# One strip of values and ones per head, and sums of the sixteen largest on VectorE, in a two-layer attention kernel

## The reference, cut to what matters

```python
# self-attention, in windows of 128 tokens
scores = jnp.einsum('bnqhd,bnkhd->bnhqk', q, k) / jnp.sqrt(jnp.float32(D))
attn = jax.nn.softmax(scores, axis=-1)
o = jnp.einsum('bnhqk,bnkhd->bnqhd', attn, v).reshape(B, L, C)
# cross-attention over the 16 largest scores of each head
top_s, top_i = jax.lax.top_k(scores, TOPK)
attn = jax.nn.softmax(top_s, axis=-1)
vg = jnp.take_along_axis(v_bh[:, :, None, :, :], top_i[..., None], axis=3)
o = jnp.einsum('bhqk,bhqkd->bqhd', attn, vg).reshape(B, L, C)
```

## Time and profile before

| | |
|---|---|
| median of 3 executions | 993.64 us |
| the profiled execution: its own time | 995.26 us |
| its span, first to last instruction | 993.2 us |
| mean granted TensorE clock | 0.979 |
| TensorE matmul busy | 899.6 us (91%) |
| VectorE busy | 755.2 us (76%) |
| ScalarE busy | 480.2 us (48%) |
| GpSimd busy | 223.9 us (23%) |

### The profile page before, as it was taken

The page is one execution under the profiler, slowest core; times in us unless marked ns, Lnnn a source line. Parts: engine busy times, 40 slices in busy tenths (PEclk is TensorE's granted clock), DMA queues, the critical chain, the costliest instruction groups (busy, mean ns, idle before and its releaser), DMA issues.

```text
span 993.2 us, 22268 instructions
## 1 busy us (share of the span) xinstructions
PE 899.6 (91%) x8160; PEld 652.8 (66%) x8160; DVE 755.2 (76%) x3952; ACT 480.2 (48%) x807; POOL 223.9 (23%) x169
## 2 busy tenths in 40 slices
PE   5978888998999899998999899998999987988997
PEld 3755656775678656775678665875668654774674
DVE  3669899897699866997589867998589865995423
ACT  3356554336462556527363556526463545534413
POOL 1226324020140405020140404111141302220101
PEclk9999998999999999999999999999999999898999
DMA  8304020000100120000100111000100100000000
GB/s 312 91 23 165 3 68 21 5 2 2 59 1 1 56 59 24 11 2 2 59 2 1 55 41 43 12 2 2 44 17 1 55 23 12 1 1 1 22 1 22
DMA packets 28651, 32.82 MB, mean 33 GB/s; under 512 B 4176, under 2 KB 25600, under 8 KB 28288
## 3 DMA queue, kind: packets, MB, share of 16 engines
q1 hardware_dynamic: 28544, 31.41, 9.9%
HBM read 25.05 MB, written 6.36 MB: 32 GB/s over the span
## 4 chain that ended last, share of the span: by engine, by line
PE 64%; DVE 23%; ACT 8%; issue 4%; DMA 1%; POOL 0%; SPq 0%; ACTq 0%; POOLq 0%
PE bank L1541 60%; DVE left L1243 6%; DVE negm L1206 5%; DVE top L1241 4%; PE bank L1743 2%; ACT hT L773 2%; PE bank L1559 2%; DVE negm L1268 2%; ACT arena L884 1%; DVE x L1180 1%; DVE stats L1122 1%; DVE xh L1134 1%; ACT arena L827 1%; DVE arena L1235 1%; DMA w_m<-in_w_ada 1%
## 5 line engine op out<-in xcount | busy, mean ns | idle before, releaser
L688 POOL TENSOR_TENSOR eS<-arena,top 128x1024 f32<-128x1024 f32 x32 | 62.0, 1939 | 276.3 <-DVE top L1241 276.3
L1541 PE MATMUL bank<-w_m,arena 128*128 128x256 f32 x512 | 112.6, 381 | 2.4 <-issue 2.4
L1541 PEld LDWEIGHTS bank<-w_m,arena 128*128 128x128 f32 x512 | 96.6, 190 | 16.8 <-issue 3.2
L1243 DVE MATCH_REPLACE8 left<-top,arena 128x64 f32<-128x64 f32 x512 | 99.8, 209 | 0.0
L1243 DVE MATCH_REPLACE8 left<-top,left 128x64 f32<-128x64 f32 x512 | 99.8, 208 | 0.0
L873 ACT ACTIVATE rden<-bank,chan 128x512 f32<-128x512 f32 x64 | 44.2, 690 | 106.5 <-PE bank L1541 106.4
L644 POOL TENSOR_SCALAR veps<-mv 128x4 f32<-128x4 f32 (+1 forms) x32 | 7.9, 247 | 366.2 <-DVE mv L1129 359.6
L827 ACT ACTIVATE arena<-bank 128x512 f32<-128x512 f32 x128 | 66.1, 602 | 46.3 <-PE bank L1541 46.3
L1206 DVE TENSOR_REDUCE negm<-bank 128x4 f32<-128x512 f32 x128 | 78.8, 681 | 12.5 <-PE bank L1541 11.7
L1241 DVE MAX8 top<-arena 128x8 f32<-128x64 f32 x512 | 67.7, 208 | 21.7 <-ACT arena L847 21.7
L1541 PE MATMUL bank<-qr,w_m 128*128 128x512 f32 x256 | 83.2, 406 | 0.2 <-ACT qr L783 0.2
(11 more groups left out here) (159 smaller groups left out, 1838.0 us busy)
## 6 DMA issues: line engine op xcount, KB each, us to landing
w_m<-in_w_m SPq DMA_DIRECT2D x4, 1024.0 KB, 5.8
xin<-in_x SPq DMA_DIRECT2D x4, 512.0 KB, 4.5
arena<-in_w_m SPq DMA_DIRECT2D x1, 2048.0 KB, 8.8
out<-x SPq DMA_DIRECT2D x4, 512.0 KB, 2.9
arena<-in_w_ada SPq DMA_DIRECT2D x1, 1536.0 KB, 10.4
gate<-gate_rows SPq DMA_DIRECT2D x12, 128.0 KB, 3.5
gated_bias<-gate_rows SPq DMA_DIRECT2D x12, 128.0 KB, 4.2
xin<-in_x SPq DMA_DIRECT2D x3, 384.0 KB, 3.1
```

The costliest lines, as they stand in the source:

```text
L688: nc.gpsimd.tensor_tensor(eS[:], S[:, t, :].rearrange("p (h n) -> p h n", h=H), top[:, :, 0:1].to_broadcast([P, H, LC]), ALU.subtract).the ...
L1243: i = nc.vector.match_replace(left[:, h, :], eight, scores, REPLACED)
L1541: return nc.tensor.matmul(dst, lhsT, rhs, start=start, stop=stop)
```

## The change

**Self-attention.** `vpad` becomes `vones`, in which each head has 16 values and 16 ones. Each of the 16 products of a window now stands by itself (no adding in pairs): it writes a strip of 32 partitions, 16 of them the weighted values and 16 the sum. The eight products with `ones_half` go, with their tile and its load. ScalarE's `self_denominator` goes. `window_divide` becomes four VectorE instructions, each waiting for the one before: a turn of 32x32 blocks of the whole bank (128x512) into `turned`, a reciprocal of the 16 sums of each query, a multiplication (128x256) into `quotient`, and a second turn (128x256) into `oT_self`. The bank counts as drained after the first turn. `project(1, a)` waits for the last turn (`s_self_out`).

**Top-k.** The sums are taken before the transposes. `exps` holds the exponentials of all 64 scores and of the 16 largest beside them, 1280 columns. A new GpSimd instruction `subtract_max_top` fills the latter after step 2, and `topk_exp` waits for both. Step 4 on VectorE first adds up the 16 (`tensor_reduce` of 128x256), inverts 16 sums, and then masks as before. A new GpSimd instruction `normalise_probs` (128x1024) multiplies the masked exponentials by the reciprocals, and only then may TensorE transpose them. In `values(2, b)` the products D go. ScalarE copies the products O to `oT` (`take_cross`), and Ln and Exp and VectorE's `cross_divide(2, b)` go. The second layer keeps its way.

**Orders.** `topk_exp(c, 1)` moves behind the fifth `silu`, `topk_exp(c, 3)` to the end of ScalarE's iteration, behind `cross_denominator(4, b)`; VectorE's `topk(c, 3, (4,))` moves behind `cross_divide(4, b)`, ahead of `window_divide(a, 3)`.

```diff
@@ window_divide, VectorE
             def window_divide(n, w):
                 key = ("PV", n, w)
-                dve.wait_ge(s_rd1, n * W + w + 1)
-                drain(nc.vector.tensor_tensor(oT_self[:, :, w * P:(w + 1) * P], ps(key)[:, 0:KC * P].rearrange("p (c n) -> p c n", c=KC),
-                                              rden_self[:, w % 2, :].rearrange("p (c n) -> p c n", c=KC), ALU.mult), key)
+                filled_wait(dve, key)
+                i = nc.vector.transpose(turned[:].rearrange("p h n -> p (h n)"), ps(key))
+                drain(i, key)
+                drained_wait(dve, key)
+                own.step(nc.vector.reciprocal(inverse[:], turned[:, :, D]))
+                own.wait()
+                own.step(nc.vector.tensor_tensor(quotient[:], turned[:, :, 0:D], inverse[:].unsqueeze(2).to_broadcast([P, H, D]), ALU.mult))
+                own.wait()
+                nc.vector.transpose(oT_self[:, :, w * P:(w + 1) * P],
+                                    quotient[:].rearrange("p (k n) d -> p k (n d)", k=KC)).then_inc(s_self_out, 1)
@@ topk, step 4, VectorE
                     if s == 4:
-                        dve.wait_ge(s_exp, n * W + t + 1)
-                        nc.vector.scalar_tensor_tensor(Sh, left[:], REPLACED, eS[:], ALU.is_equal, ALU.mult).then_inc(s_prob, 1)
+                        dve.wait_ge(s_exp, at + 1)
+                        if at:
+                            dve.wait_ge(s_prob, at)
+                        own.step(nc.vector.tensor_reduce(topk_sum[:], eS_top, AX_X, ALU.add))
+                        own.wait()
+                        nc.vector.reciprocal(topk_sum[:], topk_sum[:]).then_inc(s_sum, 1)
+                        nc.vector.scalar_tensor_tensor(Sh, left[:], REPLACED, eS, ALU.is_equal, ALU.mult).then_inc(s_masked, 1)
@@ GpSimd
+            def subtract_max_top(n, t):
+                pool.wait_ge(s_top16, n * W + t + 1)
+                nc.gpsimd.tensor_tensor(eS_top, top[:], top[:, :, 0:1].to_broadcast([P, H, TOPK]), ALU.subtract).then_inc(s_dif, 1)
+
+            def normalise_probs(n, t):
+                pool.wait_ge(s_sum, n * W + t + 1)
+                pool.wait_ge(s_masked, n * W + t + 1)
+                Sh = S[:, t, :].rearrange("p (h n) -> p h n", h=H)
+                nc.gpsimd.tensor_tensor(Sh, Sh, topk_sum[:].unsqueeze(2).to_broadcast([P, H, LC]), ALU.mult).then_inc(s_prob, 1)
@@ window_values, TensorE
                     for s in range(2):
                         for p in range(4):
-                            i = mm(ps(key)[32 * p:32 * p + 32, k * P:(k + 1) * P], vpad[:, w, 4 * k + p, 2 * D * s:2 * D * (s + 1)],
-                                   pT_self[:, w % 2, 4 * p + 2 * k + s, :], s == 0, s == 1)
-                for s in range(2):
-                    for p in range(4):
-                        i = mm(ps(key)[32 * p:32 * p + 32, KC * P:], ones_half[:, s, :],
-                               pT_self[:, w % 2, 4 * p + s:4 * p + 4:2, :], s == 0, s == 1)
+                            i = mm(out_of[32 * p:32 * p + 32, k, s], vones[:, w, 2 * (4 * k + p) + s, :],
+                                   pT_self[:, w % 2, 4 * p + 2 * k + s, :].rearrange("p (j n) -> p j n", j=RG), True, True)
@@ values, TensorE
-                    key = ("D", layer, n, k)
-                    fill_wait(pe, key)
-                    for p in range(4):
-                        i = mm(ps(key)[32 * p:32 * p + 32, :], pair_mask[:], pT[:, 4 * k + p, :], True, True)
-                    fill(i, key)
+                    if layer == 4:
+                        key = ("D", layer, n, k)
...
@@ full(a), ScalarE
                 for j in range(J):
                     silu(b, j)
-                    if j == 3:
+                    if j == 4:
                         exp_tables()
                         topk_exp(c, 1)
...
                 window(a, 1)
-                self_denominator(a, 0)
                 modulated(4, b)
                 window(a, 2)
                 last_query(b)
-                topk_exp(c, 3)
-                self_denominator(a, 1)
                 window(a, 3)
-                self_denominator(a, 2)
                 last_exps(b)
                 cross_denominator(4, b)
-                self_denominator(a, 3)
+                topk_exp(c, 3)
@@ full(a), VectorE
-                topk(c, 3, (3, 4))
+                topk(c, 3, (3,))
                 cross_divide(4, b)
+                topk(c, 3, (4,))
                 window_divide(a, 3)
```

More of the change, by code:

```diff
@@ L535, in _ @@
             load(head_select[:], t_in["head_select"], s_masks)
-            load(ones_half[:].rearrange("p s n -> p (s n)"), t_in["ones_half"], s_masks)
             load(pair_mask[:], t_in["pair_mask"], s_masks)
@@ L703, in _ @@
             layer_rstd(2, 0)
+            subtract_max_top(0, 0)
             add_bias(2, 0)
             gate_weight(1, 0)
+            normalise_probs(0, 0)
+            subtract_max(0, 1)
             add_bias(1, 1)
-            subtract_max(0, 1)
+            subtract_max_top(0, 1)
+            normalise_probs(0, 1)
             for i in range(2 * KC):
@@ L741, in _ @@
                     gate_weight(2, batch)
+                subtract_max_top(c, 3)
+                normalise_probs(c, 3)
                 layer_rstd(2, a)
@@ L747, in _ @@
             layer_rstd(3, b)
+            subtract_max_top(c, 0)
             add_bias(3, b)
+            normalise_probs(c, 0)
             subtract_max(c, 1)
+            subtract_max_top(c, 1)
+            normalise_probs(c, 1)
             subtract_max(c, 2)
+            subtract_max_top(c, 2)
+            normalise_probs(c, 2)
             subtract_max(c, 3)
@@ L807, in project_qk @@
                     biased(kT[:, k, :], ("qk", n, KC + k), CB["qk"] + KC + k)
-            def self_denominator(n, w):
-                key = ("PV", n, w)
-                filled_wait(act, key)
-                if w >= 2:
-                    drained_wait(act, ("PV", n, w - 2))
-                r = rden_self[:, w % 2, :]
-                own.step(nc.scalar.activation(r, ps(key)[:, KC * P:], ACT.Ln))
-                own.wait()
-                nc.scalar.activation(r, r, ACT.Exp, scale=-1.0).then_inc(s_rd1, 1)
             def window(n, w):
@@ L857, in take_probs, with take_cross @@
                                                    ps(key).rearrange("p (h q) -> p h q", h=4), ACT.Copy), key)
+            def take_cross(n, chunks=range(KC)):
+                for k in chunks:
+                    key = ("O", 2, n, k)
+                    filled_wait(act, key)
+                    drain(nc.scalar.activation(oT[:, k, :], ps(key), ACT.Copy), key)
             def cross_denominator(layer, n, chunks=range(KC)):
@@ L1406, in full @@
                 if a > 2:
-                    cross_divide(2, b)
                     first_moments(a)
@@ L1512, in last @@
                 last_max(b)
-                cross_divide(2, c)
                 residual_moments(2, c)
@@ L1723, in values @@
                     drained_wait(pe, ("TP", n, W - 1, k) if layer == 2 else ("B3", n, k, RG - 1))
-                    key = ("D", layer, n, k)
-                    fill_wait(pe, key)
-                    for p in range(4):
-                        i = mm(ps(key)[32 * p:32 * p + 32, :], pair_mask[:], pT[:, 4 * k + p, :], True, True)
-                    fill(i, key)
+                    if layer == 4:
+                        key = ("D", layer, n, k)
+                        fill_wait(pe, key)
+                        for p in range(4):
+                            i = mm(ps(key)[32 * p:32 * p + 32, :], pair_mask[:], pT[:, 4 * k + p, :], True, True)
+                        fill(i, key)
                     key = ("O", layer, n, k)
@@ L2133 @@
         "pair_mask": (r[:, None] // LC == np.arange(2 * D)[None, :] // D).astype(np.float32),
-        "ones_half": np.repeat(np.eye(2, dtype=np.float32), D, axis=1).reshape(1, 4 * D).repeat(P, axis=0),
     }
```

100 lines of the change are left out of this document (57 added, 43 removed).

## The result

The changed kernel takes 1025.0 us (median of 4 executions, 1022.41 to 1025.58). Beside it, on the same chip, the kernel before took 993.07 us. The ratio is 1.0315, with a 95% interval of 1.0286 to 1.0343. It is slower, and 12 us above the forecast of 1013.

The account below looks back on a forecast made before the run. It took TensorE (64% of the chain) and VectorE (23%) to bound the kernel together. Terms -11 - 1 + 20 + 7 + 7 - 3 = +19 us on 995.26 gave 1014, forecast as 1013; range 978 to 1036.

Parts of the forecast that it names:

- Costs of one: Single instructions: the new window_divide takes 1.7 us against 0.34, +1.4 per window; step 4's sum adds 0.6 per tile.
- the rival of slow turns: Window divisions: turns at their upper bound cost 0.79 us more per window, +20 us in all, 1033; chance 0.13.
- The new products: Windows' four-strip products: a rival had them not cheaper, 0.9 us more per window, at most +5, 1018; chance 0.03.
- Start of the iteration: values(2, b) to project(2, b): no products D or wait for Ln and Exp, 2.2 us gained; five iterations -11 us.
- MLP: MLP stretch: nothing lost; VectorE's two added sums (1.2 us) are covered by its 1.46 us wait there.
- Windows: Self-attention windows: VectorE's queue delays window(a, 3) by 2.2 us and project(1, a) by 3.3; six iterations +20 us.
- the block: Window division: VectorE's multiplication of SBUF operands stands still until GpSimd's normalise_probs is through, +1.0 us.
- Clock: After TensorE's gaps ahead of window(a, 3) and project(1, a): drops to 1.2 GHz cost 1.2 us per iteration, +7 us.
- Tail: Kernel's end, no windows: the projection behind cross_divide comes earlier, the last normalising stands open, -3 us.
- First two blocks and a = 2: Front: divisions, sums and waiting less a quarter of waits for ScalarE, +7, bounds 0 and +12; a = 2 -1.
- additions fit into idle time: Whole iteration: VectorE's added 8.7 us fit into 9.7 idle, so windows cost nothing, 982; chance 0.25.
- Break-even: Windows: GpSimd does not hold VectorE and the clock stays up, 995; chance 0.15.

Follow-up runs that it names:

- filler: Changed kernel plus products nobody reads, 8 ahead of window 3's scores and 3 ahead of project(1, a), in iterations a = 2 to 7: 1016.58 us, ratio 1.0275.
- max_first: Changed kernel with the maxima of half 0 moved ahead of window_divide(a, 1) on VectorE: 1023.41 us, ratio 1.0313.
- gates_first: Changed kernel with window_divide(a, 1), then the maxima of half 0, ahead of step 1 of tile 3, which goes between the maxima's halves: 1015.32 us, ratio 1.0223.
- front_doubled: Changed kernel with each window's quotient computed four times over in the first two blocks: 1034.46 us, ratio 1.0442.
- reordered: Changed kernel, VectorE reordered: window_divide(a, 0), (a, 1) and half 0's maxima, (a, 3) earlier, plus two moves in the second block: 993.26 us, ratio 0.9998.
- reordered2: As reordered, plus window_divide(a, 2) ahead of step 2 of tile 3, window_divide(1, 0) and window_max(1, 3) ahead of step 1 of tile 2: 990.83 us, 0.9986.

## Why the prediction was right, and where it was short

The direction, the range and the main mechanism held; the time came out 12 us above the forecast. Step by step:

- **Costs of one.** `window_divide` takes 1.85 us undisturbed (604.71 to 606.56, the start of the next step), forecast 1.7. The sum of step 4 costs 0.6 as forecast. The Trainium skill ("VectorE: DVE Perf Modes", The three transpose paths) has 311 ns for a turn of 128x128 in bf16; scaled by columns, that would have given an estimate of 1.24 and 0.62 us. Measured are 0.70 and 0.45, so the measurement decides against that scaling, and the rival of slow turns is out. The new products are cheap, too: the group of a window takes 1.01 us to the start of the next (580.66 to 581.67), before 0.90 and then 0.98 for the products with ones (557.55, 558.45, 559.43).
- **Start of the iteration.** Forecast 2.2 us of gain. From `values(2, b)` to `project(2, b)` it was 5.00 us (484.35 to 489.35) and is 2.79 (508.68 to 511.47): 2.2.
- **MLP.** Forecast nothing. From `project(2, b)` to the maxima scores of window 2 it was 63.20 us (489.35 to 552.55) and is 63.13 (511.47 to 574.60). It held.
- **Windows.** Forecast +2.2 us to window 3 by VectorE's queue, of it 1.0 by the block: measured 2.2 to 2.3 in five of six iterations (3.4 in a = 5, where the clock was low at 576.60), and the block was 0.97 (1.39 against 0.42). The gaps were forecast at 3.9 and 1.7 us and came out at 3.95 and 1.38. From window 3 to `project(1, a)` the forecast had 1.1 more; with the clock up, in `filler`, it is 20.21 us (587.42 to 607.63) against 19.20, +1.0. So the 3.3 us of this term held. What I had not seen is that VectorE's queue holds two of window 3's banks: the second one, freed by the turn, didn't matter for the sum but did for every remedy.
- **Clock.** Forecast 1.2 us per iteration. Without `filler`'s products the distance from window 3 to `project(1, a)` is 21.8 us and not 20.21 (363.66 to 385.49 in a = 3): 1.6. Over the trace TensorE's busy time fell by 23 us and not by 40, with 58 us more at the lower level. Together an iteration makes -2.2 + 3.3 + 1.6 = +2.7, as measured; forecast was +2.3.
- **Tail.** Forecast -3, measured -3.1.
- **First two blocks and a = 2: these terms were too small.** I wrote +7, bounds 0 and +12, and -1 for a = 2, which with the windows and the clock of a = 2 makes +10.5 up to `project(1, 2)`. Measured: +20.1, 9.6 of the 11.4 us by which the sum of +19 missed the span's 30.4. Of the 20.1 us, 12.0 lie ahead of `project(1, 1)`, where I had 7, and 8.1 in a = 2, where I had 3.5. The first figure is of one trace: the five traces whose first blocks are those of the changed kernel reach `project(1, 1)` between 129.00 and 134.09, 7 to 12 us later than before, so that part of this miss may be scatter. The second is firmer: from there to `project(1, 2)` it takes 135.87 us, 135.56 in `max_first` and 134.48 in `gates_first`, before 127.81. Three things were wrong in the terms. I let a quarter of VectorE's old waits for ScalarE (7 us) pay for the additions. But VectorE was 92% busy from 60 us to `project(1, 1)`, and its idle time there did not shrink (62.05 less 56.91 is 5.1 us before, 74.09 less 66.98 is 7.1 after): other waits took the place of those for ScalarE, and `front_doubled` shows most of the additional work coming through. I counted the clock only in the iterations; here the clock is 0.86 instead of 0.92, and `project(1, 1)` alone took 6.7 us instead of 3.7. And I put GpSimd's normalising at nothing, because GpSimd has nothing else to do there or because it ends before `probs` is due, as it does in the iterations. In a = 2 it does not: TensorE waits 4.06 us for it at 156.26, where it waited 1.46 for the masking before.

Of the rivals, "additions fit into idle time" failed for the reason given against it: the idle time was there, behind the places where the work was put. `reordered` is that rival made true by moving the work to where the idle time is; it reaches break-even, not the 982 of its forecast, because the front keeps 12 us of its loss (`project(1, 2)` at 261.83). Break-even as the prediction meant it, without a block and with the clock up, did not come: both blocks of 0.97 us and the lower clock were there.

## What to carry to other kernels

Before work is moved to an engine with idle time, find the instructions in its queue that free a buffer or a bank for the engine on the path, and put those first and the rest of their chain later; the same divisions and sums cost 3.1% in one order and nothing in another. When a wait is moved and nothing changes, look at what ends it now: products that need several banks have several gates, and the latest one decides. Price a gap with the lower clock behind it and without: here the two shares were of about the same size. Treat the filling of a pipeline apart from its steady state, for there the idle time that pays for additions in the steady state may not exist, and one trace of it can be off by several microseconds.

## What the runs showed of the hardware

- A VectorE turn of 32x32 blocks in float32 goes at the rate of a plain pass: 703 ns for 128x512 out of PSUM, 445 ns for 128x256 in SBUF, as against 681 ns for the maxima of 128x512 out of PSUM. A reciprocal of 128x16 takes 253 ns, more than the 157 ns that other tiny instructions take.
- Gaps of 3.80 to 3.95 us on TensorE were followed by the lower clock in every iteration of the changed kernel. Shorter ones were sometimes: behind the one of 1.49 us in `gates_first` at 585.24 the next products kept their times, in `reordered2` one of 1.37 us ends at 572.61, and the products at 574.52 took 2.09 us where they take 1.17. What a stretch at the lower level costs differs: in `filler`, iterations at a clock of 1.00 took 113.96 us against 115.4 to 115.7 in the changed kernel with 6.8 us at half clock; in `reordered2` an iteration with 3.4 us at half clock took 110.12 or 111.29, without any 110.11.
- Kernels with the same work in the front reached `project(1, 1)` at 134.09, 132.08 and 129.00 us, with 25, 21 and 23 us at half clock until then, and they had the first half of `project(1, 0)` at 44.91, 43.99 and 42.62. The time at half clock does not explain the order, and the cause stays open; it limits what one trace says of the front to some 5 us.
